# Smaller row steps, deeper load buffers and a re-laid projection in a graph layer, 4096 nodes, one core

## The reference

```python
h = jnp.maximum(_layernorm(x, axis=-1), 0.0)
rowsum = adj.sum(axis=1)
d_inv_sqrt = jnp.where(rowsum > 0, rowsum ** (-0.5), 0.0)
normalized_adj = d_inv_sqrt[:, None] * adj * d_inv_sqrt[None, :]
out = relu((normalized_adj @ h) @ W + b)
x = x + out
```

## Time and profile before

| | us |
|---|---|
| median of three runs | 449.1 (448.24 to 451.18) |
| the profiled execution, whole | 448.73 |
| its span, first to last instruction | 446.9 |
| PE busy | 389.5 (87%), 1632 matmul instructions |
| DVE busy | 296.0 (66%) |
| ACT busy | 262.3 (59%) |
| POOL busy | 136.7 (31%) |
| DMA, mean over the span | 330 GB/s, 147.37 MB |

### The profile page before, as it was taken

How to read it: one execution, slowest core, us unless ns; L and a number is a source line. 1 busy time by engine, 2 the same in 40 slices (tenths; PEclk the granted TensorE clock), 3 DMA queues, 4 the chain that set the end, 5 groups by cost and what they waited for, 6 DMA issues and landing times.

```text
span 446.9 us, 4679 instructions
## 1 busy us (share of the span) xinstructions
PE 389.5 (87%) x1632; PEld 306.0 (68%) x1632; DVE 296.0 (66%) x296; ACT 262.3 (59%) x225; POOL 136.7 (31%) x304
## 2 busy tenths in 40 slices
PE   0089776499999999999999999999999999999991
PEld 0077555278788878887888788878887877776660
DVE  2169567457866786678767876787778767556543
ACT  4555666567577757775777677757775733434121
POOL 3201153105510551055105510551055195333000
PEclk9999899979999999999999999999999999999996
DMA  7979999999999999999999999999999954343325
GB/s 260 377 246 352 383 352 337 405 411 394 378 385 384 392 372 382 379 397 368 400 396 381 364 406 397 391 383 370 393 401 393 351 202 162 148 177 114 122 94 188
DMA packets 26551, 147.37 MB, mean 330 GB/s; under 512 B 2720, under 2 KB 7072, under 8 KB 11168
## 3 DMA queue, kind: packets, MB, share of 16 engines
q1 hardware_dynamic: 26528, 147.07, 86.3%
HBM read 142.87 MB, written 4.19 MB: 329 GB/s over the span
## 4 chain that ended last, share of the span: by engine, by line
PE 53%; DMA 14%; POOL 10%; DVE 9%; issue 7%; ACT 6%; SPq 0%; DVEq 0%; POOLq 0%; ACTq 0%
PE pair L423 16%; PE pair L425 15%; PE pair L424 15%; DMA nat<-in_adj 10%; PE pair L443 5%; DVE lo L321 4%; ACT hi L199 4%; POOL var L258 3%; DMA at<-in_adj_t 2%; ACT nat L191 2%; DVE stats L298 2%; DVE acc L334 2%; POOL rstd L259 1%; POOL row_pow L269 1%; POOL d_wide L286 1%
## 5 line engine op out<-in xcount | busy, mean ns | idle before, releaser
L423 PE MATMUL pair<-hi,G 128*128 128x512 f32 x512 | 203.9, 398 | 47.6 <-DVE lo L321 47.6
L424 PE MATMUL pair<-lo,G 128*128 128x512 f32 x512 | 201.5, 394 | 0.0
L425 PE MATMUL pair<-hi,G 128*128 128x512 f32 x512 | 201.4, 393 | 0.0
L199 ACT CAST hi<-at 128x2048 fp32r<-128x2048 f32 (+1 forms) x72 | 123.6, 1717 | 116.4 <-PE pair L425 111.0
L321 DVE TENSOR_TENSOR lo<-at,hi 128x2048 fp32r<-128x2048 f32 (+1 forms) x72 | 147.8, 2054 | 42.7 <-ACT hi L199 42.7
L423 PEld LDWEIGHTS pair<-hi,G 128*128 128x128 f32 x512 | 97.4, 190 | 73.5 <-issue 53.7
L191 ACT ACTIVATE nat<-nat 128x2048 f32<-128x2048 f32 x64 | 122.5, 1915 | 26.2 <-DMA nat<-in_adj 26.1
L334 DVE TENSOR_TENSOR acc<-pair,acc 128x1024 f32<-128x1024 f32 x64 | 78.1, 1220 | 58.4 <-PE pair L425 58.4
L425 PEld LDWEIGHTS pair<-hi,G 128*128 128x128 f32 x512 | 97.5, 190 | 20.9
L424 PEld LDWEIGHTS pair<-lo,G 128*128 128x128 f32 x512 | 97.5, 190 | 19.6
L265 POOL TENSOR_TENSOR row_sum<-part 128x1 f32<-128x1 f32 x32 | 8.6, 270 | 120.9 <-ACT nat L191 120.9
(11 more groups left out here) (27 smaller groups left out, 124.2 us busy)
## 6 DMA issues: line engine op xcount, KB each, us to landing
nat<-in_adj SPq DMA_DIRECT2D x64, 1024.0 KB, 7.1
at<-in_adj_t SPq DMA_DIRECT2D x56, 1024.0 KB, 9.1
at<-in_adj_t SPq DMA_DIRECT2D x16, 512.0 KB, 7.9
h<-in_x SPq DMA_DIRECT2D x8, 512.0 KB, 8.5
x_out<-in_x_t SPq DMA_DIRECT2D x8, 512.0 KB, 3.3
out<-x_out SPq DMA_DIRECT2D x8, 512.0 KB, 2.6
w_sb<-in_w SPq DMA_DIRECT2D x1, 256.0 KB, 6.2
b_sb<-in_b SPq DMA_DIRECT2D x1, 1.0 KB, 5.9
```

Of the source, the lines that this page charges most:

```text
L199: nc.scalar.copy(hi[g % RING][:, 0:n, :], at[g % LA][:, 0:n, :]).then_inc(hi_ready, 1)
L423: nc.tensor.matmul(into[:, f, :], big, hi[g % RING][:, t, :], start=(t == 0), stop=False)
L424: nc.tensor.matmul(into[:, f, :], big, lo[g % RING][:, t, :], start=False, stop=False)
L425: mm = nc.tensor.matmul(into[:, f, :], small, hi[g % RING][:, t, :], start=False, stop=(j == end - 1))
```

## The change

The contraction goes in 16 equal steps of 2 tiles. A load of adj_t, and with it a cast and a subtract, covers two panels of 2 tiles (a slot g, four to a step, 1 MB and 24 matmuls as a full group had). `nat` and `at` have four buffers each; x_out and result lie in the nat buffers. Panels 0 and 1 stay in PSUM from the first step to the last (`held`), the six others go through two PSUM buffers (`moved`) and are added to acc by DVE once per step. The centring of x is a Relu with bias on ACT, one tile at a time, behind every second sum_nat. In the projection acc is stationary and W moves (8 matmuls of 256 columns per panel), so that the output rows stand on partitions: d is then a scalar per partition, and the transposes of d, POOL's widening, ACT's copies and ACT's last Relu are gone. x and out are stored so that each partition's part is contiguous.

```diff
+SW = 2
+SLOT_PANELS = 2
+TILES = SW * SLOT_PANELS
...
+    STEPS = NB // SW
+    LAST = STEPS - 1
+    SLOTS = NP // SLOT_PANELS
+    NATS = 2 * SW // SLOTS
+    HELD = 2
+    LN = 4
+    LA = 4
     RING = 2
-    PAIRS = 3
+    ROT = 2
+    MOVED = NP - HELD
...
+        x_out = [nat[e][:, 0:BW * D].rearrange("p (t f) -> p t f", f=D) for e in range(LN)]
+        result = [nat[e][:, BW * D:2 * BW * D].rearrange("p (t f) -> p t f", f=D) for e in range(LN)]
+
+        held = [ps(f"held{e}", [P, FD, PW]) for e in range(HELD)]
+        moved = [ps(f"moved{e}", [P, FD, PW]) for e in range(ROT)]
...
+            def load_slot(g):
                 at_least(sp, lo_ready, g - LA + 1)
-                sp.dma_start(at[g % LA][:, 0:end - first, :],
-                             adj_t[first // BW, i, :, t:t + end - first, :]).then_inc(at_landed[g % LA], DMA)
+                sp.dma_start(at[g % LA][:, :, :], adj_t[g]).then_inc(at_landed[g % LA], DMA)
...
+                for q in range(SLOTS):
+                    load_slot(SLOTS * k + q)
+                    for m in nats_after(k, q):
                         load_nat(m)
+            sp.wait_ge(nat_summed, 2 * NB)
+            for i in range(LN):
+                sp.dma_start(x_out[i], x[i]).then_inc(x_out_landed[i], DMA)
             for i in range(NP):
                 sp.wait_ge(out_ready, i + 1)
...
+                sp.dma_start(out[i], x_out[i % LN]).then_inc(stored[i % LN], DMA)
+                if i + LN < NP:
+                    sp.wait_ge(stored[i % LN], DMA)
+                    sp.dma_start(x_out[i % LN], x[i + LN]).then_inc(x_out_landed[i % LN], DMA)
...
+            def round_slot(g):
                 act.wait_ge(at_landed[g % LA], DMA * (g // LA + 1))
...
+                at_least(act, panel_done, slot_done(g - RING))
+                nc.scalar.copy(hi[g % RING][:, :, :], at[g % LA][:, :, :]).then_inc(hi_ready, 1)
+
+            def centre(j):
+                own = h[j // BW % 2][:, j % BW, :]
+                act.wait_ge(rstd_ready, j // BW + 1)
+                nc.scalar.activation(own, own, ACT.Relu, bias=minus_mean[:, j:j + 1]).then_inc(h_ready, 1)
+
+            for j in range(SW):
+                for c in range(2):
+                    sum_nat(2 * j + c)
+                centre(j)
+            for k in range(STEPS):
+                for q in range(SLOTS):
+                    round_slot(SLOTS * k + q)
+                    for m in nats_after(k, q):
                         sum_nat(m)
...
+                        if m % 2:
+                            centre(m // 2)
...
             def moments(c):
                 tiles = slice(c * BW, (c + 1) * BW)
                 pool.wait_ge(stats_made, BW * (c + 1))
-                at_least(pool, h_ready, BW * c)
                 then(nc.gpsimd.tensor_tensor(out=mean2[:, :], in0=stats[:, :, 1], in1=stats[:, :, 4], op=ALU.add))
-                nc.gpsimd.tensor_scalar(mean[:, tiles], mean2[:, :], 0.5, None, ALU.mult)
+                nc.gpsimd.tensor_scalar(minus_mean[:, tiles], mean2[:, :], -0.5, None, ALU.mult)
...
+            def gather(k, i):
+                n = MOVED * k + i - HELD
+                dve.wait_ge(panel_done, NP * k + i + 1)
                 if k == 0:
-                    nc.vector.tensor_copy(acc[:, i, :, :], from_pair[:, :, :]).then_inc(pair_taken, 1)
+                    nc.vector.tensor_copy(acc[:, i, :, :], moved[n % ROT][:, :, :]).then_inc(taken, 1)
                 else:
...
+                    dve.wait_ge(taken, n - MOVED + 1)
+                    nc.vector.tensor_tensor(out=acc[:, i, :, :], in0=moved[n % ROT][:, :, :], in1=acc[:, i, :, :],
+                                            op=ALU.add).then_inc(taken, 1)
...
+            def finish(i):
+                e = i % LN
+                half = BW // 2
+                for a in range(2):
+                    dve.wait_ge(w_done, 2 * i + a + 1)
+                    for t in range(half):
+                        tile = half * a + t
+                        nc.vector.scalar_tensor_tensor(
+                            out=result[e][:, tile, :], in0=held[i % HELD][:, a, t * D:(t + 1) * D],
+                            scalar=d[:, BW * i + tile:BW * i + tile + 1], in1=b_sb[:, :], op0=ALU.mult,
+                            op1=ALU.add).then_inc(scaled, 1)
+                dve.wait_ge(scaled, BW * (i + 1))
+                dve.wait_ge(x_out_landed[e], DMA * (i // LN + 1))
+                nc.vector.scalar_tensor_tensor(out=x_out[e], in0=result[e], scalar=0.0, in1=x_out[e], op0=ALU.max,
+                                               op1=ALU.add).then_inc(out_ready, 1)
...
+                for q in range(SLOTS):
+                    g = SLOTS * k + q
+                    if fresh is not None and q == 0:
+                        take_stats(fresh)
+                    for i in range(SLOT_PANELS * q, SLOT_PANELS * (q + 1)):
+                        if i >= HELD:
+                            gather(k, i)
+                    if q == SLOTS - 1:
+                        for m in nats_after(k, q):
                             if m % 2:
                                 make_G(m // 2)
                     subtract(g + 2)
...
+                    if q < SLOTS - 1:
+                        for m in nats_after(k, q):
                             if m % 2:
                                 make_G(m // 2)
+            dve.wait_ge(b_landed, DMA)
...
+                    n = MOVED * k + i - HELD
+                    into = moved[n % ROT]
+                    at_least(pe, taken, n - ROT + 1)
...
+                    t = i % SLOT_PANELS * SW + c
                     if i == 0:
                         pe.wait_ge(G_ready, j + 1)
-                    t = j - first
+                    begins = c == 0 and (i >= HELD or k == 0)
+                    ends = c == SW - 1 and (i >= HELD or k == LAST)
...
             def project(i):
...
+                half = BW // 2
+                pe.wait_ge(total_ready, min(i + 1, HELD))
+                at_least(pe, taken, MOVED * LAST + i - HELD + 1 if i >= HELD else 0)
+                at_least(pe, scaled, BW * (i - HELD + 1))
+                for a in range(2):
+                    for t in range(half):
+                        tile = half * a + t
+                        for f in range(FD):
+                            mm = nc.tensor.matmul(held[i % HELD][:, a, t * D:(t + 1) * D],
+                                                  acc[:, i, f, tile * P:(tile + 1) * P], w_sb[:, f, :],
+                                                  start=(f == 0), stop=(f == FD - 1))
```

More of the change, by code:

```diff
@@ L25, in at_least, with build @@
         eng.wait_ge(sem, value)
-def build(nc, x, adj, adj_t, x_t, w, b, out):
-    N, D = x.shape
+def build(nc, x, adj, adj_t, w, b, out):
+    N, D = adj.shape[0], w.shape[0]
     NB = N // P
@@ L274, in scale_of @@
                                         op=ALU.mult).then_inc(s_ready, 1)
-            for first, end in STEPS:
-                if first % BW == 0:
-                    moments(first // BW)
-                for j in range(first, end):
+            for k in range(STEPS):
+                if fresh_x(k) is not None:
+                    moments(fresh_x(k))
+                for j in range(SW * k, SW * (k + 1)):
                     scale_of(j)
-            for i in range(NP):
-                at_least(pool, d_turned, i - 1)
-                for t in range(BW):
-                    j = BW * i + t
-                    wide = nc.gpsimd.tensor_scalar(d_wide[i % 2][:, t, :], ones[:, :], d[:, j:j + 1], None, ALU.mult)
-                    if t < BW - 1:
-                        then(wide)
-                    else:
-                        wide.then_inc(d_wide_ready, 1)
         @block.vector
@@ L354, in _ @@
             take_stats(0)
-            centre(0)
-            for j in range(STEPS[0][1]):
+            for j in range(SW):
                 make_G(j)
@@ L369, in _ @@
                     subtract(g + 2)
-                    if fresh is not None and i == 0:
-                        take_stats(fresh)
-                    if fresh is not None and i == 1:
-                        centre(fresh)
-                    if i < NP - 1:
-                        for m in chunks_after(k, i):
+                    if q < SLOTS - 1:
+                        for m in nats_after(k, q):
                             if m % 2:
                                 make_G(m // 2)
+            dve.wait_ge(b_landed, DMA)
@@ L378, in _ @@
             for i in range(NP):
-                g = NP * LAST + i
-                gather(g)
-                if g + 2 < GROUPS:
+                if i < HELD:
+                    take_held(i)
+                else:
+                    gather(LAST, i)
+                g = SLOTS * LAST + i // SLOT_PANELS
+                if i % SLOT_PANELS == SLOT_PANELS - 1 and g + 2 < SLOTS * STEPS:
                     subtract(g + 2)
                 if i >= 1:
-                    scale(i - 1)
-                if i >= 2:
```

(15 more changed lines are left out.)

217 lines of the change are left out of this document (42 added, 175 removed).

## The result

The changed kernel takes **462.3 us** (median of 4 runs, 461.41 to 463.8) against 450.1 us for the kernel before on the same chip: 1.0295 times as long, 95% interval 1.0248 to 1.0342. 457 was forecast, 442 to 468 the range.

The account below looks back on a forecast made before the run. TensorE was taken to bound the old loop with 0.8 us to spare. Start 22.0, slow clock 1.7, matmuls 347.9, stops 45.3, projections 28.6 and end 5.5 gave 451.0; clock drops made 456, time beyond the span 457.8; forecast 457, range 442 to 468.

Parts of the forecast that it names:

- The three stops: TensorE waits: 0.98 us in panel 0 every step; 0.32 at panel 4 and 0.79 at panel 6 even; 3.10 at panel 4 odd.
- The sum, 45.3: All TensorE stops over the run: 15 x 0.98 + 8 x (0.32 + 0.79) + 7 x 3.10 us.
- the 451.0 of the sum: Start, slow clock at the start, matmuls, stops, projections and end together, in us, before further clock drops.
- The chain of the odd step: Statistics, rstd, centring, cast, subtract, gather 2 in turn before panel 4; ACT's cast 2.8 us late, stop 3.10 us.
- The clock: TensorE's clock falls after three of the seven 3.1 us stops, 1.7 us lost each, 5 us; bounds none and 12 us.
- case 1: Stops as walked, with 0 to 5 lost clock drops: 452 to 461 us, chance 0.57.
- all seven stops lose clock: Rival: every odd-step stop drops TensorE's clock, or each hand-over is 0.1 us longer: 464 us, chance 0.15.
- The counterexample at 69.40: In the kernel before, TensorE stood for 3.27 us there and its clock stayed at 1.00.
- 1 to 2 us of slack per step: DMA hidden: 8.65 MB a step takes 22.8 us at 380 GB/s, against a step of 24.8 us.
- Start, projection, end: First matmul at about 22.0 us; projection 28.6 us with weight loads hidden; end after the last projection 5.5 us.
- rival 5: The change does what its parts say without new waits, TensorE without stops: 408 us, chance 0.05.

Follow-up runs that it names:

- e4_order: Changed kernel with the odd-step centring moved behind a later cast and both tiles' G made earlier on DVE: 413.2 us, 0.9211 of the kernel before.
- e3_warm: Changed kernel with 20 matmuls of zeros filling the long stop before panel 4 in odd steps, all waits kept: 452.9 us, 1.0095 of the kernel before.
- e1_late_centre: Changed kernel with ACT's first centring in odd steps moved behind the cast of slot 4k+3: 440.7 us, 0.981 of the kernel before.
- e6_pow: Changed kernel in which POOL computes rstd twice, lengthening the chain: 475.1 us, 1.0576 of the kernel before.
- e5_order_shallow: e4_order with the buffer depths of the kernel before (two nat, three at, two x_out): 416.1 us, 0.9264 of the kernel before.
- e7_before_deep: Kernel before the change with four nat buffers instead of two, at keeping its three: 439.8 us, 0.9804 of the kernel before.
- e2_early_G: Changed kernel with the second tile's G made on DVE ahead of gathers 6 and 7: 461.5 us, 1.0286 of the kernel before.
- e8_early_warm: e2_early_G with 28 matmuls of zeros in the stop before panel 4 of odd steps: 445.9 us, 0.993 of the kernel before.

## Why the prediction was right

- **The bound.** TensorE bound the old loop with 0.8 us to spare, and the order around it decided. e4_order shows how much hangs on the order: the changed kernel's work, unchanged, keeps TensorE 99.7% busy in it.
- **The three stops.** Forecast from one matmul's start to the next, beyond its turn: 0.98, 0.32, 0.79 and 3.10 us. Measured 0.90, 0.23, 0.65 and 2.92, and to each come 0.11 us by which the second matmul after a restart is late (at 98.48 the first shows 0.50 us, and the second starts at 98.81, 0.33 later instead of 0.23). The sum, 45.3, is right within 1 us, and e3_warm, which takes only the clock away, spans 451.3 against the 451.0 of the sum. That it is as close as 0.3 us is in part luck: I had the start 0.6 and the end 0.2 us too long, and small terms elsewhere make that up.
- **The chain of the odd step** is as walked: `var` in 0.20 us while DVE is idle, rstd 4.57 us after the statistics began, the centring 0.51 instead of 0.42, the cast 2.8 us late as forecast. e1_late_centre and e6_pow show it by shortening and lengthening it.
- **The clock** is the term that was mis-sized. I took 3 falls of 1.7 us, 5 us; there were 6 of 1.45, 8.7 us. With that the sum is 459.7, and the span 460.0. The time lies between two cases: case 1 (0.57) ended at 461 with five drops, and "all seven stops lose clock" (0.15) gave 464. The counterexample at 69.40, a stop of 3.27 us without a fall, led me to one in two. The kernel before had a third stop of this kind that I did not use: after the 6.15 us before 90.45 a matmul took 0.63 us, and its clock was low for 6.8 us. Two in three would have been about five drops. The Trainium skill, "TensorE: Matmul & The Clock Gate", section "A second HAM failure mode: psum-queue depth-cycling", tells of a kernel with cycling PSUM buffers whose clock goes back and forth. The trace agrees in that, but the falls came after the one long stop of an odd step, never after the short ones.
- **DMA.** I wrote 1 to 2 us of slack per step by 380 GB/s. It gave 416 to 420 as long as it was behind the earlier trace rows. The 380 of the middle was what the kernel before asked for (17.3 MB in 44.8 us), not what DMA can give: e4_order drew 411 from 100 to 200 us. The limit of about 358 GB/s in the Trainium skill, "DMA: Bandwidth & Descriptors", section "Where 436 GB/s comes from", worked out there as half of a stack's 716 GB/s for each of two cores, did not bind this kernel, which runs on one: these 420 are above it.
- **Start, projection, end.** First matmul 21.4 (22.0). Projection 28.8 us (28.6): the weight loads hide, at 190 ns each. From TensorE's last instruction to the end 5.3 us (5.5).
- **What I left unused.** The walk showed that the longest stop was one instruction in the wrong place on ACT. It could have said that the change is worth 8% with the order mended. The prediction's rival 5, TensorE without stops, had that price (408 us) and 0.05; e4_order shows 413.2.

What stays open: why the kernel before drew only 332 to 366 GB/s in its starved stretch when e5_order_shallow, with the same depths, had 422. Four nat buffers brought it to 349 to 406 (e7_before_deep), so the depth is part of it there. Its adj_t loads there are half as long per partition and its steps uneven; none of the runs separates these. Open too is what decides which stop is followed by a fall of the clock, and how long it lasts: the length of the stop alone does not.

## What to carry to other kernels

Halving a loop's step halves the time in which work beside it has to be ready: the last tile's G was due 4 us into the step and now 1.4. When steps shrink or work moves to another engine, walk one step of each in-order queue with durations from the trace, and ask of every wait what stands behind it; then move the waiting instruction, which costs nothing. Count a stop's clock with it: with a stop of 3 us the engine here lost half as much again (1.45 us), with one of 4 us 2.4.

## What the runs showed of the hardware

- In the changed kernel a stop of 2.74 us idle was followed by 3.4 us at 1.2 GHz in six of seven cases; in e2_early_G one of 3.80 by 6.8 us in seven of seven; in e6_pow one of 3.85 by 3.4 us in four cases and by 6.8 in three. Stops of up to 0.74 us never were. In the kernel before, those of 1.05 to 1.66 us and one of 3.27 were not, one of 2.84 was by 3.4 us and one of 6.15 by 6.8. Filling the stop with matmuls of zeros kept 2.4 GHz (e3_warm, e8_early_warm).
- The restarts with a fall came 51.2 to 51.4 us apart in the changed kernel (111.05, 162.41, 213.75, 264.97, 316.17, 367.38), though the one pair of steps without a fall took 49.8: once it had fallen, it fell in every pair.
- Every restart of TensorE at the full clock in the changed kernel and its variants, however short the stop, put the second matmul 0.11 us late: the first shows 0.50 us instead of 0.39. In the kernel before it was 0.08, the first showing 0.47.
- One core drew 420 GB/s from HBM over 78 us, from 22 to 100 us of e4_order, with loads of 1 MB, 8 KB per partition.
